# One decoder layer on one core: the mix of attention values as three passes of split values

## The chip, the cores and the metric

The kernel runs on one core of a Trainium2 chip. The metric is the device time of one execution in microseconds (us); less is better. The kernel before takes 398.93 us, the median of three runs (398.75 to 399.02).

## The reference, cut to what matters

One decoder layer for 8 sequences of 128 tokens with 512 features: a Mamba-2 mixer with a gated MLP (inner width 1792), attention of each sequence over its own context of 128 keys, and a base matrix with a routed low-rank addition. A layer norm stands behind each of the three parts.

```python
def _L0_xattn_ref(query, key):
    a = jnp.einsum('bqd,bkd->bqk', query, key)
    e = jax.nn.softmax(a, axis=-1)
    c = jnp.einsum('bqk,bkd->bqd', e, key)
    return c
x = _layernorm(x + mamba_and_mlp(x))
x = _layernorm(x + _L0_xattn_ref(x, ctx_4096))
x = _layernorm(x + _L0_ffn_ref(x, ...))
```

(The first of the three norms is abridged: `mamba_and_mlp` is the call of `_L0_attn_ref`.) The change touches only the last einsum of the attention: 128 queries by 128 keys, times 128 keys by 512 features, once for each sequence.

## The kernel before, in words

One sequence (128 tokens by 512 features) is one tile; there are 8, numbered 0 to 7. The kernel is written engine by engine, with the order of each engine's instructions by hand and with semaphores between them. No planner moves anything. It has three stages: the mixer, gate and up of the MLP, and the **down loop** (the last third of the span), the only stage that the change touches.

Large products run as **three passes**. A value in 32 bits is split into a high part, its rounding to the type fp32r (ScalarE copies it), and a low part, the value less the high part (VectorE or GpSimd subtracts). TensorE then adds high by low, high by high and low by high into one bank of PSUM, one instruction each (`three_pass`, L646 to L648). A product whose operands are plain 32-bit values is one call in the code and takes two matrix instructions in the trace.

The down loop is software-pipelined over the tiles. Each engine has a function `tail(t, par, ...)`; this text calls one pass through it **step t**. In step t TensorE works on three tiles at once, in this order:

- `down(t, ..., 0)`: the down projection of tile t, inner blocks 0 to 7, 24 instructions. Before it TensorE waits for `hid_lo` (both parts of the hidden values of tile t are there).
- `turn_x1(t-1)` (L882): four transposes of the normed result of tile t-1, after the semaphore `ln_out[0]` from VectorE.
- `turn_x2(t-2)`, two more blocks of down, `attend(t-1)` (L902, the scores), two more blocks.
- `base(t-2)` (base matrix and routing logits), `turn_ex(t-1)` (L908, transposes the exponentials), block 12 of down.
- `turn_z(t-2)` (L958), **`mix(t-1)`** (L913, the values), block 13 of down, `lora(t-2)` (L964, L966).

ScalarE in step t computes the reciprocal deviations for the norms (L1363, L1365), copies the turned tiles out of PSUM (L1373, L1377), makes the high part of the hidden values of tile t+1 (`split_hid`, L1356), then takes the exponential (`exp_scores`, L1387), copies its transpose (L1390) and copies the turned routing values (L1394).

VectorE in step t runs in this order:

- `add_mlp(t-1)` (L1846) and moments, `add_ffn(t-3)` (L1855, L1856), `normed(0, t-1)` (L1804, which releases `turn_x1(t-1)` of the next entry on TensorE's list), the third norm of tile t-3, `lo_of_x2(t-2)` (L1882)
- `row_max(t-1)` (L1893), then `route(t-2)`, seven small instructions (L1810 to L1837)
- `split_hid(t+1)` (L1791, the low part of the hidden values: releases `hid_lo`)
- `add_attention(t-1)` (L1898, L1901: waits for the mix), moments and norm of its result (L1797, L1799, L1804)

Step 0 has only down. Step 1 has no routing and no base (f is False there), step 2 has all but the third norm, and steps 3 to 6 are full; 3 to 6 are a hardware loop on TensorE and ScalarE, 5 and 6 on VectorE. Step 7, written out, is drawn together: its down projection is cut by `END_SEGS` instead of `SEGS`, so that only five blocks (15 instructions) stand ahead of `turn_x1(6)`, and four blocks behind `mix(6)`.

```python
SEGS = ((0, 8), (8, 10), (10, 12), (12, 13), (13, 14))
END_SEGS = ((0, 5), (5, 6), (6, 8), (8, 9), (9, 13), (13, 14))
```

The context of tile t comes by two DMAs into the place of its hidden values, issued by SyncE when these are split (L481, L482): the turned keys, and 512 words further the keys as they are, which serve as values.

The functions that the diff touches:

Of the kernel before, what the change touches and what calls it, by code (L numbers as in the profile page):

```python
# [132 lines left out]
def build(nc, x, ctx, ctxT, wstream, conv_w, conv_b, a_log, d_skip, dt_bias, ln1_w, ln2_w,  # L133
          gate_lora, expert_bias, lora_b, out):
    es = ExitStack()
    with es:
        def sb(name, shape, dt=F32):
            return es.enter_context(nc.sbuf_tensor(name, shape, dt))

        def sem(name):  # L140
            return es.enter_context(nc.semaphore(name))
# [7 lines left out]
        def at(name, word, shape, dt=F32):  # L149
# [25 lines left out]
                    rawS[:, 3 * CH:4 * CH].rearrange("p (s n) -> p s n", s=2))  # L175
        x2S = x2_parts[0]
        rows = sb("rows", [P, B, D])
        big = sb("big", [P, NM * TOK])
        tmp = sb("tmp", [P, 7 * D])

        sums = side[:, 0:CH]
        sg = tmp[:, 0:4 * D].rearrange("p (k n) -> p k n", k=4)
# [32 lines left out]
        x2T = tmp[:, 2560:3072]  # L215
        ex = tmp[:, 3072:3200]
        exT = tmp[:, 3200:3328]
        zm = tmp[:, 3328:3456]
        stats = tmp[:, 3456:3474].rearrange("p (k s) -> p k s", k=3)
        lg = tmp[:, 3488:3488 + 3 * E].rearrange("p (k e) -> p k e", k=3)  # L220
# [74 lines left out]
        ln_u, ln_st, ln_mv, ln_log, ln_rs, ln_out = (  # L295
            [sem(f"ln{i}_{what}") for i in (1, 2, 3)] for what in ("u", "st", "mv", "log", "rs", "out"))
        q_ps, q_ok, sc_ps, mx_ok, ex_ok = sem("q_ps"), sem("q_ok"), sem("sc_ps"), sem("mx_ok"), sem("ex_ok")
        rinv_ok, exT_ps, exT_ok, pv_ps = sem("rinv_ok"), sem("exT_ps"), sem("exT_ok"), sem("pv_ps")
        raw_max, scaled = sem("raw_max"), sem("scaled")
        x2_ps, x2_ok, x2_hi, x2_lo = sem("x2_ps"), sem("x2_ok"), sem("x2_hi"), sem("x2_lo")  # L300
# [87 lines left out]
        def base_w(part, c):  # L388

            return base_end if part * DC + c == 2 * DC - 1 else baseS[:, part * DC + c, :]  # L390

        def context(t):

# [257 lines left out]
        def _(pe):  # L651
# [255 lines left out]
                pe.wait_ge(ex_ok, t + 1)  # L907
                pe.transpose(bank[4][:, P:2 * P], ex, ident[:, :]).then_inc(exT_ps, 1)  # L908

            def mix(t):  # L910
                pe.wait_ge(exT_ok, t + 1)
                _, key = context(t)
                pe.matmul(bank[5][:, :], exT, key, start=True, stop=True).then_inc(pv_ps, 1)  # L913
# [58 lines left out]
            def tail(t, par, d=True, a=True, f=True, first_d=False, first_f=False):  # L972

                if d:
                    down(t, par, 0, first_d)
                if a:
                    turn_x1(t - 1)
                if f:
                    turn_x2(t - 2, par)
                if d:  # L980
                    down(t, par, 1, first_d)
                if a:
                    attend(t - 1, 1 - par)
                if d:
                    down(t, par, 2, first_d)
                if f:
                    base(t - 2, first_f)
                if a:
                    turn_ex(t - 1)
                if d:  # L990
                    down(t, par, 3, first_d)
                if f:
                    turn_z(t - 2)
                if a:
                    mix(t - 1)
                if d:
                    down(t, par, 4, first_d)
                if f:
                    lora(t - 2)
# [15 lines left out]
            down(last, 1, 2, False, END_SEGS)  # L1015
            turn_ex(last - 1)
            down(last, 1, 3, False, END_SEGS)
            mix(last - 1)
            down(last, 1, 4, False, END_SEGS)
            turn_x2(last - 1, 0)  # L1020
            down(last, 1, 5, False, END_SEGS)
# [13 lines left out]
            mix(last)  # L1035
# [15 lines left out]
        def _(act):  # L1051
# [315 lines left out]
            def store(t):  # L1367
                act.wait_ge(ln_out[2], t + 1)
                act.dma_start(out[bass.ds(t, 1)].rearrange("a p n -> (a p) n"), u3).then_inc(stored, 16)
# [15 lines left out]
            def exp_scores(t, scale=1.0):  # L1385
# [4 lines left out]
                act.activation(exT, bank[4][:, P:2 * P], ACT.Copy).then_inc(exT_ok, 1)  # L1390
# [6 lines left out]
            def tail(t, par, a=True, f=True, g=True, split=True, first_split=False):  # L1397

                if a:
                    rstd(0, t - 1)  # L1400
                if g:
                    rstd(2, t - 3)
                if a:
                    copy_q(t - 1)
                if f:
                    hi_of_x2(t - 2)
                if split:
                    split_hid(t + 1, 1 - par, first_split)
                if g:
                    store(t - 3)  # L1410
                if a:
                    exp_scores(t - 1)
                if f:
                    copy_z(t - 2)
                if a:
                    rstd(1, t - 1)
# [3 lines left out]
            bw_high(0)  # L1420
            bw_high(1)
            route_high()
            tail(1, 1, f=False, g=False)
            tail(2, 0, g=False)
            with act.Fori(1, B // 2 - 1) as j:
                tail(2 * j + 1, 1)
# [4 lines left out]
            copy_q(last - 1)  # L1431
            hi_of_x2(last - 2)
            store(last - 3)
            exp_scores(last - 1)
# [5 lines left out]
            exp_scores(last, scale=lrs[:, 0:1])  # L1440
            rstd(2, last - 2)
            rstd(1, last)
            copy_halves(last, x2T, x2_ps, (3, 5), x2_ok)
# [11 lines left out]
        def _(v):  # L1455
# [435 lines left out]
            def row_max(t):  # L1891
                v.wait_ge(sc_ps, t + 1)
                v.tensor_reduce(sm[:, 0:1], bank[4][:, 0:P], AX.X, ALU.max, negate=True).then_inc(mx_ok, 1)  # L1893

            def add_attention(t, par):

                v.wait_ge(ex_ok, t + 1)
                v.reciprocal(sm[:, 2:3], sm[:, 1:2]).then_inc(rinv_ok, 1)  # L1898
                v.wait_ge(rinv_ok, t + 1)
                v.wait_ge(pv_ps, t + 1)  # L1900
                v.scalar_tensor_tensor(out=u2[:, par, :], in0=bank[5][:, :], scalar=sm[:, 2:3], in1=u1,  # L1901
                                       op0=ALU.mult, op1=ALU.add).then_inc(ln_u[1], 1)

            def tail(t, par, a=True, f=True, g=True, split=True, first_g=False):

                if a:
                    add_mlp(t - 1, 1 - par)
                    moments(0, t - 1, u1)
                if g:
                    add_ffn(t - 3, 1 - par, stored_tiles=None if first_g else t - 3)  # L1910
                if a:
                    normed(0, t - 1, u1)
                if g:
                    moments(2, t - 3, u3)
                    normed(2, t - 3, u3)
                if f:
                    lo_of_x2(t - 2)
                if a:
                    row_max(t - 1)
                if f:  # L1920
                    route(t - 2)
                if split:
                    split_hid(t + 1, 1 - par)
                if a:
                    add_attention(t - 1, 1 - par)
                    moments(1, t - 1, u2[:, 1 - par, :])
                    normed(1, t - 1, u2[:, 1 - par, :])
# [19 lines left out]
            normed(2, last - 3, u3)  # L1947
            lo_of_x2(last - 2)
            row_max(last - 1)
            add_attention(last - 1, 0)  # L1950
            moments(1, last - 1, u2[:, 0, :])
            normed(1, last - 1, u2[:, 0, :])
# [84 lines left out]
```

## Time and profile before

| what | us |
|---|---|
| median of three runs | 398.93 |
| the profiled execution, its own time | 400.36 |
| its span, first to last instruction | 398.6 |
| TensorE busy in the span | 383.1 |
| VectorE busy | 293.0 |
| ScalarE busy | 191.2 |
| GpSimd busy | 135.0 |

The profile lists for each engine the start and the duration of every instruction, and where the engine was idle before it, what ended the idle time. The matrix instructions of TensorE overlap: a 512-column pass is listed with some 0.39 us, and the next one starts some 0.23 us after it. So the distance between starts is what counts there. On VectorE and ScalarE an instruction may be listed as starting slightly before its forerunner ends.

### The profile page before, as it was taken

How to read it: one execution, taken by the hardware profiler on the slowest of the kernel's cores; microseconds unless marked ns; L12 is line 12 of the kernel's file. 1: busy time of each engine (PE TensorE's matmuls, PEld its weight loads, DVE VectorE, ACT ScalarE, POOL GpSimd, SP SyncE). 2: the span in 40 equal slices, each digit the busy share in tenths (PEclk: the TensorE clock that was granted, in tenths of full speed). 3: DMA queues.
4: the chain of work that ended last, by engine and by line, in shares of the span. 5: the costliest groups of instructions: out<-in, count | busy, mean ns of one | idle time of the engine just before them, and what ended most of it. 6: DMA issues, size and time to landing. Idle time of an engine off the chain costs nothing.

```text
span 398.6 us, 5321 instructions
## 1 busy us (share of the span) xinstructions
PE 383.1 (96%) x1891; PEld 310.2 (78%) x1891; DVE 293.0 (74%) x514; ACT 191.2 (48%) x385; POOL 135.0 (34%) x121
## 2 busy tenths in 40 slices
PE   7999999999899999999999999999999999998994
PEld 3778787766579988888888888888788888896773
DVE  2589996277775888979797979696655857658587
ACT  5678465866755566152524243863234144143141
POOL 2504222844644674647382827840000000000000
PEclk9999999999999999999999999999999999999998
DMA  7801531110001023121212111352102102101002
GB/s 262 285 38 53 156 118 46 53 54 0 1 2 53 3 87 125 53 57 50 72 38 102 37 72 53 115 178 78 54 7 74 53 26 79 53 26 54 28 0 81
DMA packets 12979, 27.63 MB, mean 69 GB/s; under 512 B 1841, under 2 KB 2225, under 8 KB 12954
## 3 DMA queue, kind: packets, MB, share of 16 engines
q1 hardware_dynamic: 12090, 25.87, 19.5%
q10 hardware_dynamic: 864, 1.44, 1.0%
q8 instruction: 14, 0.23, 0.3%
q14 instruction: 11, 0.09, 0.1%
HBM read 25.20 MB, written 2.11 MB: 69 GB/s over the span
## 4 chain that ended last, share of the span: by engine, by line
PE 80%; DVE 8%; ACT 6%; POOL 3%; issue 2%; DVEq 0%; ACTq 0%; POOLq 0%
PE bank L646 23%; PE bank L648 22%; PE bank L647 22%; PE bank L762 2%; PE bank L902 2%; PE bank L913 2%; PE bank L657 1%; POOL sets L551 1%; PE bank L685 1%; DVE tmp L1797 1%; DVE big L1566 1%; ACT big L1138 1%; ACT big L1063 1%; DVE tmp L1609 1%; PE bank L918 1%
## 5 line engine op out<-in xcount | busy, mean ns | idle before, releaser
L646 PE MATMUL bank<-sets,station 128*128 128x512 f32 (+1 forms) x424 | 164.9, 389 | 2.7 <-DVE sets L1591 1.1
L647 PE MATMUL bank<-sets,station 128*128 128x512 f32 (+1 forms) x424 | 158.5, 374 | 0.0
L648 PE MATMUL bank<-sets,station 128*128 128x512 f32 (+1 forms) x424 | 158.5, 374 | 0.0
L646 PEld LDWEIGHTS bank<-sets,station 128*128 128x128 f32 x424 | 79.9, 188 | 20.0 <-issue 4.2
L647 PEld LDWEIGHTS bank<-sets,station 128*128 128x128 f32 x424 | 80.0, 189 | 14.8 <-issue 2.2
L648 PEld LDWEIGHTS bank<-sets,station 128*128 128x128 f32 x424 | 79.8, 188 | 14.6
L604 POOL TENSOR_TENSOR big<-tmp,side_f 128x512 f32<-128x512 f32 x17 | 26.4, 1567 | 23.8 <-DVE side_f L1670 23.8
L1363 ACT ACTIVATE small<-small 128x1 f32<-128x1 f32 x24 | 7.1, 296 | 50.2 <-DVE small L1799 50.2
L509 POOL TENSOR_TENSOR station<-raw,station 128x1024 fp32r<-128x1024 f32 x7 | 16.8, 2396 | 40.0 <-ACT station L1055 40.0
L1670 DVE TENSOR_TENSOR side_f<-side_f,bank 128x512 f32<-128x512 f32 x36 | 24.6, 685 | 3.9 <-PE bank L648 3.5
L1523 DVE SCALAR_TENSOR_TENSOR big<-bank,cw,big 128x508 f32<-128x508 f32 (+2 forms) x36 | 26.2, 740 | 1.4 <-ACT big L1115 0.3
L1654 DVE TENSOR_TENSOR station<-raw,station 128x512 fp32r<-128x512 f32 (+1 forms) x24 | 20.6, 898 | 6.1 <-ACT station L1254 6.1
L1670 DVE TENSOR_TENSOR tmp<-tmp,bank 128x512 f32<-128x512 f32 x30 | 20.4, 682 | 3.2 <-PE bank L648 3.2
L1254 ACT ACTIVATE station<-raw 128x512 fp32r<-128x512 f32 x12 | 7.5, 625 | 29.6 <-PE bank L648 29.6
L1664 DVE TENSOR_TENSOR station<-side_f,station 128x512 fp32r<-128x512 f32 x24 | 19.4, 813 | 3.2 <-ACT station L1277 3.2
L1277 ACT ACTIVATE station<-side_f 128x1024 fp32r<-128x1024 f32 x12 | 12.7, 1059 | 13.9 <-POOL side_f L596 13.9
L647 PE MATMUL bank<-side,rawS 128*128 128x274 f32 (+1 forms) x60 | 17.7, 296 | 0.0
L648 PE MATMUL bank<-side,rawS 128*128 128x274 f32 (+1 forms) x60 | 17.7, 296 | 0.0
L1804 DVE TENSOR_SCALAR tmp<-tmp,small 128x512 f32<-128x512 f32 x21 | 11.4, 545 | 8.4 <-ACT small L1365 8.4
L1797 DVE BATCH_NORM_STATS2 tmp<-tmp 128x6 f32<-128x512 f32 x24 | 16.6, 693 | 0.6
L591 POOL TENSOR_TENSOR side_f<-raw 128x256 f32<-128x256 f32 x12 | 9.1, 754 | 20.3 <-DVE station L1664 20.3
L1791 DVE TENSOR_TENSOR station<-big,station 128x1792 fp32r<-128x1792 f32 x7 | 14.1, 2017 | 0.0
(206 smaller groups left out, 657.8 us busy)
## 6 DMA issues: line engine op xcount, KB each, us to landing
raw<-wstream SPq DMA_DIRECT2D x31, 512.0 KB, 3.4
rows<-x SPq DMA_DIRECT2D x8, 256.0 KB, 4.5
big<-ctxT SPq DMA_DIRECT2D x8, 256.0 KB, 2.6
big<-ctx SPq DMA_DIRECT2D x8, 256.0 KB, 2.9
out<-tmp ACTq DMA_DIRECT2D x5, 256.0 KB, 2.0
decays<-step_rows SPq DMA_DIRECT2D x4, 256.0 KB, 3.5
big<-step_rows SPq DMA_DIRECT2D x4, 256.0 KB, 5.2
out<-tmp SPq DMA_DIRECT2D x2, 256.0 KB, 2.2
```

The source lines that it names most:

```text
L509: pool.tensor_tensor(dst, raw[:, raw_slot(n), :], hi.bitcast(F32), ALU.subtract).then_inc(w_lo, 1)
L604: pool.tensor_tensor(hid_block(m, hf), blocks(sg[:, k, :]), blocks(value), ALU.mult).then_inc(up_ok, 1)
L646: pe.matmul(ps, a_hi, b_lo, start=first, stop=False)
L647: pe.matmul(ps, a_hi, b_hi, start=False, stop=False)
L648: return pe.matmul(ps, a_lo, b_hi, start=False, stop=last)
L1277: act.activation(groupS[:, buf, 0, D + HALF_K:7 * HALF_K], sums, ACT.Copy).then_inc(g_hi, 1)
L1523: v.scalar_tensor_tensor(out=dst[:, :, s:L], in0=src[:, :, 0:L - s], scalar=cw[:, m, 3 - s:4 - s], in1=dst[:, :, s:L], op0=ALU.mult, op1=A ...
L1654: v.tensor_tensor(groupS[:, buf, 1, lo:hi], src, groupS[:, buf, 0, lo:hi].bitcast(F32), ALU.subtract) \
L1664: v.tensor_tensor(groupS[:, buf, 1, q], sums[:, bass.ts(k, D)], groupS[:, buf, 0, q].bitcast(F32), ALU.subtract).then_inc(g_lo, 1)
L1670: v.tensor_tensor(dst, other, product_bank(g, n), op).then_inc(done, 1)
L1791: v.tensor_tensor(hidS[:, par, 1, :], big[:, bass.ds(t * (NM * P), NM * P)], hidS[:, par, 0, :].bitcast(F32), ALU.subtract).then_inc(hid_l ...
L1797: v.bn_stats(stats[:, k, :], u).then_inc(ln_st[i], 1)
```

## The change

In steps 1 to 7 the mix of tiles 0 to 6 becomes three passes. `mix_last` is the old `mix`, for tile 7.

- ScalarE: `high_key(t-1)` copies the values (128x512) as their high part into raw slot 0, ahead of `exp_scores`. At its first use it waits until that slot is read out (`bw_lo`). The copy of the turned exponentials (L1390 before) now writes the high part of them.
- VectorE: `low_key(t-1)` behind `row_max` puts the low part of the values in place of the values themselves (128x512). `low_of_exT(t-1)` subtracts the high part from the turned exponentials in PSUM (128x128) and puts the low part where the exponentials stood; it waits for ScalarE's copy (`exT_ok`) and stands ahead of `split_hid`, behind `route` where there is one.
- TensorE: `mix` waits for `key_lo` and `exT_ok`, runs two passes, waits for `exT_lo`, and runs the third.

```diff
+            def high_key(t, par, first_use=False):
+                if first_use:
+                    act.wait_ge(bw_lo, 5)
+                act.wait_ge(ctx_in[par], 16 * (t + 2 - par))
+                _, key = context(t)
+                act.activation(key_high(par), key, ACT.Copy).then_inc(key_hi, 1)
...
+            def low_key(t, par):
+                v.wait_ge(key_hi, t + 1)
+                _, key = context(t)
+                v.tensor_tensor(key_low(t), key, key_high(par).bitcast(F32), ALU.subtract).then_inc(key_lo, 1)
+
+            def low_of_exT(t):
+                v.wait_ge(exT_ok, t + 1)
+                v.tensor_tensor(exT_parts[1], bank[4][:, P:2 * P], exT_parts[0].bitcast(F32), ALU.subtract).then_inc(exT_lo, 1)
...
                 if a:
                     row_max(t - 1)
+                    low_key(t - 1, 1 - par)
                 if f:
                     route(t - 2)
+                if a:
+                    low_of_exT(t - 1)
                 if split:
                     split_hid(t + 1, 1 - par)
...
-            def mix(t):
+            def mix(t, par):
+                pe.wait_ge(key_lo, t + 1)
+                pe.wait_ge(exT_ok, t + 1)
+                pe.matmul(bank[5][:, :], exT_parts[0], key_low(t), start=True, stop=False)
+                pe.matmul(bank[5][:, :], exT_parts[0], key_high(par), start=False, stop=False)
+                pe.wait_ge(exT_lo, t + 1)
+                pe.matmul(bank[5][:, :], exT_parts[1], key_high(par), start=False, stop=True).then_inc(pv_ps, 1)
+
+            def mix_last(t):
                 pe.wait_ge(exT_ok, t + 1)
                 _, key = context(t)
                 pe.matmul(bank[5][:, :], exT, key, start=True, stop=True).then_inc(pv_ps, 1)
...
@@ step 7, VectorE
             row_max(last - 1)
+            low_key(last - 1, 0)
+            low_of_exT(last - 1)
             add_attention(last - 1, 0)
```

`exT_parts` are the places of `exT` (high) and `ex` (low), `key_low(t)` the place of the values in the context of tile t, `key_high(par)` a half of raw slot 0.

## Rows read from the trace of the kernel before

**Rows 1.** Windows: busy us of each engine, PE clock granted, DMA share, GB/s.
```profile
319.30:335.10 15.80, 15.80 (x89) 13.44 (x88) 10.45 (x25) 5.07 (x13) 0.00 (x0) 1.00 0.14 50
...
364.00:367.00 3.00, 1.50 (x10) 1.01 (x9) 2.90 (x8) 0.50 (x2) 0.00 (x0) 1.00 0.03 10
...
394.00:398.00 4.00, 0.00 (x0) 0.00 (x0) 2.03 (x5) 0.50 (x2) 0.00 (x0) 0.73 0.37 131
```

**Rows 2.** Chain that ended last, 325 to 337 us: start, us, what.
```profile
327.96 0.86 PE bank L913 x2
328.82 0.23 PE bank L646
```

**Rows 3.** Timeline of TensorE, step 4 into 5: start, us, what.
```profile
326.88 0.27 PE L908 MATMUL bank<-ident,tmp 128*128 128x128 f32 x1
...
327.80 1.02 PE L913 MATMUL bank<-big,tmp 128*128 x2
...
329.60 0.40 PE L646 MATMUL bank<-sets,station 128*128 128x512 f32 x1
...
335.12 0.60 PE L882 MATMUL bank<-ident,tmp 128*128 128x128 f32 x4
```

**Rows 4.** Timeline of VectorE, step 4 into 5; idle before it in brackets.
```profile
325.55 0.16 DVE L1810 TENSOR_TENSOR tmp<-bank,eb 128x4 f32<-128x4 f32 x1 [2.61 <-PE bank L648]
...
326.90 0.19 DVE L1837 TENSOR_TENSOR tmp<-tmp 128x32 fp32r<-128x32 f32 x1
327.01 2.02 DVE L1791 TENSOR_TENSOR station<-big,station 128x1792 fp32r<-128x1792 f32 x1
...
331.43 0.55 DVE L1804 TENSOR_SCALAR tmp<-tmp,small 128x512 f32<-128x512 f32 x1 [0.60 <-ACT small L1365]
331.89 0.68 DVE L1846 TENSOR_TENSOR tmp<-bank,rows 128x512 f32<-128x512 f32 x1
...
334.12 0.55 DVE L1804 TENSOR_SCALAR tmp<-tmp,small 128x512 f32<-128x512 f32 x1
```

**Rows 5.** Timeline of ScalarE, step 4.
```profile
322.97 0.37 ACT L1387 ACTIVATE tmp<-bank,small 128x128 f32<-128x128 f32 x1 [0.17 <-DVE small L1893]
...
327.19 0.28 ACT L1390 ACTIVATE tmp<-bank 128x128 f32<-128x128 f32 x1 [3.75 <-PE bank L908]
```

**Rows 6.** Groups by line and form: count, busy us, mean ns.
```profile
L1888 DVE TENSOR_TENSOR rawS<-bank,rawS 128x256 fp32r<-128x256 f32 x2 | 0.8, 419 | 0.3 <-ACT rawS L1445 0.3
...
L1254 ACT ACTIVATE station<-raw 128x512 fp32r<-128x512 f32 x12 | 7.5, 625 | 29.6 <-PE bank L648 29.6
```

**Rows 7.** Line L1694: ns min/median/max, first and last start.
```profile
L1694 DVE TENSOR_TENSOR rawS<-raw,side x1: 684/684/684, 271.7 to 271.7; 128x512 fp32r<-128x512 f32 x1
```

**Rows 8.** Timeline of VectorE, step 1 into 2.
```profile
278.61 0.29 DVE L1893 TENSOR_REDUCE small<-bank 128x1 f32<-128x128 f32 x1 [3.28 <-PE bank L902]
278.82 2.02 DVE L1791 TENSOR_TENSOR station<-big,station 128x1792 fp32r<-128x1792 f32 x1
...
281.74 0.75 DVE L1901 SCALAR_TENSOR_TENSOR tmp<-bank,small,tmp 128x512 f32<-128x512 f32 x1 [0.83 <-PE bank L913]
...
286.73 0.55 DVE L1804 TENSOR_SCALAR tmp<-tmp,small 128x512 f32<-128x512 f32 x1 [0.60 <-ACT small L1365]
```

**Rows 9.** Timeline of ScalarE, step 1.
```profile
280.11 0.28 ACT L1390 ACTIVATE tmp<-bank 128x128 f32<-128x128 f32 x1 [0.71 <-PE bank L908]
```

**Rows 10.** Timeline of TensorE, steps 2 and 7.
```profile
287.64 0.60 PE L882 MATMUL bank<-ident,tmp 128*128 128x128 f32 x4
...
366.37 0.66 PE L882 MATMUL bank<-ident,tmp 128*128 128x128 f32 x4 [1.50 <-DVE tmp L1804]
...
371.42 1.02 PE L913 MATMUL bank<-big,tmp 128*128 128x512 f32 x2
```

**Rows 11.** Timeline of VectorE, step 7.
```profile
365.77 0.55 DVE L1804 TENSOR_SCALAR tmp<-tmp,small 128x512 f32<-128x512 f32 x1
...
372.55 0.75 DVE L1901 SCALAR_TENSOR_TENSOR tmp<-bank,small,tmp 128x512 f32<-128x512 f32 x1 [2.14 <-PE bank L913]
```

More of the change, by code:

```diff
@@ L177, in build @@
         rows = sb("rows", [P, B, D])
+        big_at = -(-nc.sbuf_base // 32) * 32
         big = sb("big", [P, NM * TOK])
+        bigS = nc.alloc_sbuf_tensor_at("bigS", [P, NM * TOK], F32R, offset=big_at)
+        tmp_at = -(-nc.sbuf_base // 32) * 32
         tmp = sb("tmp", [P, 7 * D])
+        tmpS = nc.alloc_sbuf_tensor_at("tmpS", [P, 7 * D], F32R, offset=tmp_at)
         sums = side[:, 0:CH]
@@ L217, in build @@
         exT = tmp[:, 3200:3328]
+        exT_parts = (tmpS[:, 3200:3328], tmpS[:, 3072:3200])
         zm = tmp[:, 3328:3456]
@@ L297, in build @@
         q_ps, q_ok, sc_ps, mx_ok, ex_ok = sem("q_ps"), sem("q_ok"), sem("sc_ps"), sem("mx_ok"), sem("ex_ok")
+        key_hi, key_lo, exT_lo = sem("key_hi"), sem("key_lo"), sem("exT_lo")
         rinv_ok, exT_ps, exT_ok, pv_ps = sem("rinv_ok"), sem("exT_ps"), sem("exT_ok"), sem("pv_ps")
@@ L390, in base_w, with key_high, key_low @@
             return base_end if part * DC + c == 2 * DC - 1 else baseS[:, part * DC + c, :]
+        def key_high(par):
+            return rawS[:, bass.ts(par, D)]
+        def key_low(t):
+            return bigS[:, bass.ds(t * (NM * P) + D, D)]
         def context(t):
@@ L994, in tail @@
                 if a:
-                    mix(t - 1)
+                    mix(t - 1, 1 - par)
                 if d:
@@ L1017, in _ @@
             down(last, 1, 3, False, END_SEGS)
-            mix(last - 1)
+            mix(last - 1, 0)
             down(last, 1, 4, False, END_SEGS)
@@ L1034, in _ @@
             base_half(0, 1, x2_parts[1], (2,))
-            mix(last)
+            mix_last(last)
             base_half(0, 1, x2_parts[1], (3,))
@@ L1383, in copy_halves, with exp_scores @@
                     act.activation(dst[:, bass.ts(i, 2 * P)], bank[banks[i]][:, 0:2 * P], ACT.Copy).then_inc(done, 1)
[L1385 removed]
+            def high_key(t, par, first_use=False):
[4 more added lines that the diff above has]
+                act.activation(key_high(par), key, ACT.Copy).then_inc(key_hi, 1)
+            def exp_scores(t, scale=1.0, last=False):
                 act.wait_ge(mx_ok, t + 1)
@@ L1389, in exp_scores @@
                 act.wait_ge(exT_ps, t + 1)
-                act.activation(exT, bank[4][:, P:2 * P], ACT.Copy).then_inc(exT_ok, 1)
+                act.activation(exT if last else exT_parts[0], bank[4][:, P:2 * P], ACT.Copy).then_inc(exT_ok, 1)
             def copy_z(t, bk=3):
@@ L1395, in copy_z, with tail @@
                     .then_inc(zmT_ok, 1)
-            def tail(t, par, a=True, f=True, g=True, split=True, first_split=False):
+            def tail(t, par, a=True, f=True, g=True, split=True, first_split=False, first_key=False):
                 if a:
@@ L1411, in tail @@
                 if a:
+                    high_key(t - 1, 1 - par, first_key)
                     exp_scores(t - 1)
@@ L1422, in _ @@
             route_high()
-            tail(1, 1, f=False, g=False)
+            tail(1, 1, f=False, g=False, first_key=True)
             tail(2, 0, g=False)
@@ L1433, in _ @@
             store(last - 3)
+            high_key(last - 1, 0)
             exp_scores(last - 1)
@@ L1439, in _ @@
             copy_z(last - 2, bk=2)
-            exp_scores(last, scale=lrs[:, 0:1])
+            exp_scores(last, scale=lrs[:, 0:1], last=True)
             rstd(2, last - 2)
```

## The prediction

> **What bounds the kernel now.** I read the windows first. In a full step of the down loop TensorE is busy for all of its 15.80 us at a granted clock of 1.00, its upper level of 2.4 GHz; VectorE is busy for 10.45 us and ScalarE for 5.07 us [rows 1]. The chain of waits agrees: between 325 and 337 us it is TensorE alone, and the old mix has 0.86 us in it, a pass of down 0.23 us [rows 2]. So a first look says: TensorE bounds, and shortening the mix pays.
>
> The second look must go to the thing that the busy shares hide, the order of VectorE's work. TensorE turns the exponentials at 326.88 and wants the normed tile for `turn_x1` at 335.12 [rows 3]. Between these lies a chain on ScalarE and VectorE. VectorE finishes the routing at 327.09 (326.90 + 0.19) and works through twelve instructions, from the split of the hidden values at 327.01 to the norm that ends at 334.67 (334.12 + 0.55), idle only for the 0.60 us of the deviation that ScalarE computes; `add_mlp` at 331.89 waits for nobody [rows 4]. A norm is handed to TensorE in 0.05 us: in step 7 it ends at 366.32 [rows 11], and the transposes start at 366.37 [rows 10]. So in a full step VectorE is early by only 335.12 - 334.67 - 0.05 = 0.40 us. In step 7, where five blocks of down stand ahead of `turn_x1` and not eight, TensorE already waits 1.50 us for it [rows 10]: VectorE has no room there at all. What the change does to this chain decides the time.
>
> **TensorE: the mix.** It goes from 0.86 us to three passes of 0.23 us, 0.70 us with rounding, as passes behind one another run everywhere here [rows 2]. That saves 0.16 us in each of seven mixes. Ends: nothing, if the waits inside hold it up; 0.17 us, if they don't. The wait for `exT_lo` should not: the mix starts at 327.80 [rows 3], its third pass is due 0.46 us later, at 328.26, and the subtraction ends by 327.79 (next part). In steps where TensorE then waits for VectorE the saving is worth nothing, since the chain starts at `turn_ex`, which stands ahead of the mix.
>
> **ScalarE: the high part of the values.** 128x512 from SBUF takes 0.63 us [rows 6]. It stands behind the split of the hidden values and ahead of the exponential, which was waiting 0.17 us at 322.97 [rows 5]; the exponential comes some 0.4 us later, and `turn_ex` is not due before 326.88 [rows 3], so 3 us cover it. Cost 0; without this cover, 0.4 us a step. The values have landed by then, since the scores of the same tile, from the same pair of DMAs, were already taken. In step 1 the slot is free, as VectorE was done with the base weights before its first norm. No DMA is added or moved; the copy of the turned exponentials only changes its target type.
>
> **VectorE: the low part of the values.** 128x512 takes 0.68 us [rows 7]. In a full step VectorE is idle for 2.61 us ahead of the routing [rows 4], so it costs 0. In step 7 it falls into the wait for the mix, 2.14 us [rows 11]: 0. In step 1 it stands ahead of a wait that is longer anyway (below).
>
> **VectorE: the low part of the exponentials.** This is the expensive edit. Not its length: 128x256 from PSUM takes 0.42 us [rows 6], so 128x128 is some 0.29 us, and as neighbours overlap by 0.08 us (326.90 + 0.19 against 327.01 [rows 4]), 0.21 us from start to start. It is the wait in front of it. It needs ScalarE's copy, which ends at 327.19 + 0.28 = 327.47 [rows 5], while VectorE could start the split of the hidden values at 327.01. Behind the waiting instruction stand the split, the attention sum, three norms: all of the chain above. The split now starts at 327.47 + 0.03 + 0.21 = 327.71, 0.70 us late.
>
> A rule of the Trainium skill speaks further against it ("VectorE: DVE Perf Modes", The DRAIN you can't avoid): a VectorE instruction does not start before the pipe of the one ahead is empty, so one should count instructions and not semaphores. The row shows an overlap of 0.08 us at this very place [rows 4], so I do not charge the drain in full; by the rule it would.
>
> Now the sum, by the place where TensorE waits.
>
> - Steps 3, 4, 5 and 6 (behind the mixes of steps 2 to 5): VectorE is 0.70 us late against a room of 0.40 us, so `turn_x1` is 0.30 us late, four times: 1.20 us. The split ends at 329.73 as well, later than TensorE wants it for the first block of down (329.60 [rows 3], now 0.16 earlier). It waits there about 0.3 us, and the 24 passes that follow then reach `turn_x1` at about 335.3, just ahead of the norm at 335.42. These two waits are one, not two.
> - Step 2 (behind step 1): there is no routing in step 1, so before, the split started at 278.82, directly after the row maximum. It now waits for the copy of the turned exponentials, which ends at 280.39 [rows 9], and starts at 280.63: 1.81 us late. Of this 0.80 us is taken up by the time that VectorE stood waiting for the mix (0.83 less a usual gap of 0.03 [rows 8]), which leaves 1.01. The norm ended at 287.28 [rows 8], `turn_x1` began at 287.64 [rows 10]: room 0.31. Cost 0.70 us.
> - Step 7 (behind step 6): no room. Cost 0.70 us.
> - The mix of step 7: VectorE waited for it (2.14 us) and what follows waits for VectorE [rows 11]. Behind `turn_ex` of step 7 the low part of the exponentials is done by the third pass, as above: the mix starts at 371.42 [rows 10], its saving counts. -0.16 us.
>
> Together 0.70 + 1.20 + 0.70 - 0.16 = 2.44 us. A TensorE that has been kept waiting needs a little to start: the four transposes take 0.66 us after a wait and 0.60 us without [rows 10, 3]. That is up to 0.06 us at five new waits, 0.30 us together. I take the middle: +2.6 us. The profiled execution (400.36 us, span 398.6) would become about 403.0 with a span of 401.2; on the median of 398.93 us it makes **401.5 us**.
>
> Ends: if the subtraction starts and ends 0.1 us sooner at each of six places and no start-up is paid, +1.84. If each of the six costs its full length and another 0.1 us of handover, with start-up, 2.74 + 6 x 0.18 = +3.8. So this case has 400.8 to 402.7.
>
> **The rivals.**
>
> - The pipe's drain is paid in full. The split then starts 0.08 us later at six places, +0.5 us: 402.0 us. Against it: the overlap in rows 4, between two small instructions. For it: the subtraction is larger than these. This is the rule of the skill's page named above.
> - TensorE keeps the bound and the mix pays everywhere: 7 x 0.16 = 1.1 us less, 397.8 us, on the other side of no change. The mechanism is the room at `turn_x1`: it decides at a delay of 0.40 us of the split in full steps. Only if more than 0.70 us of VectorE's chain could be made up does it hold; for it speaks that TensorE was at 100% [rows 1] and the chain of waits names no other engine [rows 2]; against it the twelve instructions with only 0.60 us of idle time [rows 4].
> - Half of it: if the copy of the turned exponentials were ready by the end of the routing (0.38 us sooner than in rows 5), the delay would be only 0.21 us; full steps would gain 0.16 each and the other terms eat that, within 0.5 us of no change: 399.2 us.
> - Only the ends cost: the full steps absorb the delay, steps 2 and 7 do not. +0.70 + 0.70 - 0.16 = 1.24, 400.2 us.
> - The three passes don't do what they should, because the wait for `exT_lo` holds the third: then the mix of step 7 gains nothing, and 401.7 us result. The margin of 0.47 us speaks against it.
> - TensorE's clock falls in the longer waits. In step 7 the idle time grows from 1.50 to 2.2 us. With 1.50 us idle in a stretch of 3 us the granted clock stayed 1.00; it fell to 0.73, part of the stretch at the lower level of 1.2 GHz, where TensorE had nothing for 4 us at the end [rows 1]. If it fell in step 7, the 5 us of work up to the mix would take up to twice as long: 406 us.
>
> **How the numbers follow.** Chances: the forecast 0.65, the drain 0.12, the ends only 0.06, the mix without a gain 0.03, the clock 0.03, TensorE keeps the bound 0.06, the half case 0.05. Faster by over 0.2% (0.8 us, about what can be told from no change) is then 0.06, within it 0.05, slower 0.89. The range reaches from 400.5, a little below the likeliest case's own low end, to 402.8; the ends-only case, the clock and the cases on the other side lie outside, with 0.2.
>
> **What would show it.** Right: VectorE idle about 0.4 us behind L1837 until ScalarE's copy in steps 2 to 6, and about 1 us or more in step 1; new waits of TensorE of 0.2 to 0.4 us for `hid_lo` or `ln_out` in each step from 2 to 6; 2.2 us instead of 1.50 at `turn_x1` in step 7; full steps of 16.1 us and not 15.8; the three passes 0.23 us apart. Wrong: full steps of 15.8 us or less, no wait of TensorE in them, or the subtraction beginning before the routing.

## The result, and the profile after

The changed kernel takes 402.46 us (median of four runs, 401.82 to 402.99) against 398.84 us before (median of four, 398.53 to 399.02): slower by 3.6 us, ratio 1.008 (95% interval 1.0058 to 1.0103). The forecast was 401.5 us in a range of 400.5 to 402.8.

In single executions of every kernel here, changed or not, the start of the kernel is short or some 2 us longer (the first transposes of the down loop begin near 273.8 or near 275.6 us), so profiles are compared from these transposes on, and not by their spans.

From there to the last instruction the kernel before takes 398.6 - 275.69 = 122.9 us and the changed one 400.5 - 273.64 = 126.9 us. Of the 3.95 us of difference, 2.7 us are those of the forecast, term by term (see the point-by-point account below). The rest, 1.2 us, is a fall of TensorE's clock in step 7, a rival to which I had given a chance of 0.03.

First VectorE of the changed kernel, step 4 into 5 (columns: start, us, what, idle time before it and what ended it). L1868 is the end of the routing, L1933 the new subtraction, L1822 the split of the hidden values, L1835 the norm; they answer to [rows 4].

```profile
326.34 0.19 DVE L1868 TENSOR_TENSOR tmp<-tmp 128x32 fp32r<-128x32 f32 x1
326.94 0.29 DVE L1933 TENSOR_TENSOR tmpS<-bank,tmpS 128x128 fp32r<-128x128 f32 x1 [0.41 <-ACT tmpS L1419]
327.15 2.02 DVE L1822 TENSOR_TENSOR station<-big,station 128x1792 fp32r<-128x1792 f32 x1
...
334.25 0.55 DVE L1835 TENSOR_SCALAR tmp<-tmp,small 128x512 f32<-128x512 f32 x1
```

The routing ends at 326.53 and the split starts at 327.15. Before, it overlapped the routing's end by 0.08 us [rows 4]. So it is 0.70 us late: 0.41 us of pure waiting and 0.29 us for the subtraction. TensorE in the same step, which answers to [rows 3]:

```profile
326.32 0.27 PE L922 MATMUL bank<-ident,tmp 128*128 128x128 f32 x1
...
327.13 0.27 PE L980 MATMUL bank<-ident,tmp 128*128 128x128 f32 x1
327.16 0.49 PE L927 MATMUL bank<-bigS,tmpS 128*128 x1
327.49 0.40 PE L928 MATMUL bank<-rawS,tmpS 128*128 128x512 f32 x1
327.73 0.40 PE L930 MATMUL bank<-rawS,tmpS 128*128 128x512 f32 x1
327.96 0.40 PE L660 MATMUL bank<-sets,station 128*128 128x512 f32 x1
328.19 0.39 PE L661 MATMUL bank<-sets,station 128*128 128x512 f32 x1
...
329.22 0.50 PE L660 MATMUL bank<-sets,station 128*128 128x512 f32 x1 [0.17 <-DVE station L1822]
...
334.86 0.66 PE L896 MATMUL bank<-ident,tmp 128*128 128x128 f32 x4
```

The same two neighbours of the mix in the kernel before, `turn_z` ahead of it and the second pass of the block behind it (starts of the passes right beside the old mix are listed unevenly, so I take these):

```profile
327.69 0.27 PE L958 MATMUL bank<-ident,tmp 128*128 128x128 f32 x1
...
328.89 0.40 PE L647 MATMUL bank<-sets,station 128*128 128x512 f32 x1
```

The three passes (L927, L928, L930) run without a gap, and the third does not wait. Between the two neighbours it is 328.19 - 327.13 = 1.06 us, before 328.89 - 327.69 = 1.20 us: 0.14 us saved, where 0.16 was forecast. The saving is real, and TensorE then gives it away twice. At 329.22 it waits for the split of the hidden values: from the second pass of the block to this pass it is 1.03 us (329.22 - 328.19), before 0.71 (329.60 - 328.89), 0.32 us more. And its transposes take 0.66 us instead of 0.60, the mark of having waited. From turned exponentials to `turn_x1` it is 8.54 us, before 8.24 [rows 3].

Windows of step 7 (length, then busy us of PE, PEld, DVE, ACT, POOL, then the granted clock, DMA share and GB/s), and TensorE's marks there, which answer to [rows 10]:

```profile
362.00:365.00 3.00, 3.00 (x15) 2.37 (x13) 2.33 (x5) 0.50 (x2) 0.00 (x0) 1.00 0.53 171
365.00:368.00 3.00, 1.06 (x8) 0.78 (x7) 2.88 (x8) 0.50 (x2) 0.00 (x0) 0.96 0.03 10
368.00:371.00 3.00, 3.00 (x13) 2.71 (x12) 1.24 (x2) 2.10 (x5) 0.00 (x0) 0.50 0.24 90
371.00:374.00 3.00, 3.00 (x16) 2.42 (x15) 1.25 (x4) 0.73 (x3) 0.00 (x0) 0.97 0.00 0
```

```profile
361.59 0.50 PE L660 MATMUL bank<-sets,station 128*128 128x512 f32 x1 [0.17 <-DVE station L1822]
...
367.22 0.66 PE L896 MATMUL bank<-ident,tmp 128*128 128x128 f32 x4 [1.94 <-DVE tmp L1835]
...
372.74 0.27 PE L922 MATMUL bank<-ident,tmp 128*128 128x128 f32 x1
```

The wait ahead of `turn_x1` grew from 1.50 to 1.94 us. That is less than the 0.76 us by which the step became longer, because TensorE comes to it later as well: at 361.59 it has already waited for the split of the hidden values. Behind the 1.94 us a window of three microseconds ran at 0.50 of full speed, 1.2 GHz, TensorE's lower level; the windows around it were granted 0.96 and 0.97, so that the lower level lasted a little over 3 us. From `turn_x1` to `turn_ex` it is 5.52 us; before, 4.25 (366.37 to 370.62).

### The profile page after: what moved, and what is told of

It reads as the page before. It is cut to its first block, busy times and chain, and to the rows that moved or that the text cites. A ratio compares the mean times of both kernels' runs of the same rounds, so it can differ in the third digit from the quotient of the medians.

```text
span 400.5 us, 5370 instructions
## 1 busy us (share of the span) xinstructions
PE 382.5 (95%) x1898; PEld 310.9 (78%) x1898; DVE 299.4 (75%) x528; ACT 193.9 (48%) x392; POOL 134.9 (34%) x121
## 4 chain that ended last, share of the span: by engine, by line
PE 75%; DVE 11%; ACT 6%; POOL 3%; issue 3%; DMA 1%; SPq 0%; DVEq 0%; ACTq 0%; POOLq 0%
PE bank L660 23%; PE bank L662 22%; PE bank L661 22%; DVE station L1822 3%; PE bank L916 2%; DMA rows<-x 1%; POOL sets L565 1%; ACT big L1085 1%; DVE big L1597 1%; PE bank L699 1%; PE bank L896 1%; PE bank L940 1%; DVE tmp L1828 1%; DVE tmp L1640 1%; PE bank L671 1%
## 5 line engine op out<-in xcount | busy, mean ns | idle before, releaser
L1835 DVE TENSOR_SCALAR tmp<-tmp,small 128x512 f32<-128x512 f32 x21 | 11.4, 544 | 8.4 <-ACT small L1387 8.4
L1822 DVE TENSOR_TENSOR station<-big,station 128x1792 fp32r<-128x1792 f32 x7 | 14.1, 2015 | 0.0
```

The source lines that it names most:

```text
L1822: v.tensor_tensor(hidS[:, par, 1, :], big[:, bass.ds(t * (NM * P), NM * P)], hidS[:, par, 0, :].bitcast(F32), ALU.subtract).then_inc(hid_l ...
```

## The experiments

All times of a kernel are medians. Ratios are against the kernel before in the same round, estimated over the executions, and are not the quotient of the two medians. The table (us) is worked out from the starts of the four transposes `turn_x1` in each profiled execution: "step 2" is the distance from those of step 1 to those of step 2, and so on. "Rest" reaches from those of step 7 to the end of the span, "down loop" from the first of them to the end. In the last row the transposes of steps 1 to 6 stand one block (0.70 us) later than in the others.

| kernel | step 2 | steps 3 to 6, mean | step 7 | rest | down loop |
|---|---|---|---|---|---|
| before | 11.95 | 15.82 | 15.43 | 32.2 | 122.9 |
| changed | 12.64 | 16.19 | 16.19 | 33.3 | 126.9 |
| changed, again | 12.64 | 16.19 | 16.20 | 32.0 | 125.6 |
| changed, filled wait | 12.65 | 16.20 | 16.18 | 32.0 | 125.7 |
| before, filled wait | 11.94 | 15.82 | 15.43 | 32.2 | 122.9 |
| subtraction alone, waiting | 12.65 | 16.18 | 16.18 | 32.2 | 125.8 |
| subtraction alone, not waiting | 11.94 | 15.82 | 15.64 | 32.2 | 123.0 |
| two passes | 11.70 | 15.50 | 15.50 | 33.0 | 122.2 |
| two passes, filled wait | 11.69 | 15.48 | 15.47 | 31.8 | 120.9 |
| split ahead of the transposes | 12.44 | 15.80 | 15.42 | 32.4 | 123.4 |
| GpSimd, behind the transposes | 12.84 | 16.86 | 16.29 | 32.0 | 128.6 |
| GpSimd, ahead of them | 11.95 | 15.77 | 15.44 | 32.4 | 122.8 |
| changed, one block more | 12.97 | 16.07 | 15.42 | 32.0 | 124.7 |

### Is it the subtraction behind ScalarE's copy? (the kernel before, plus that instruction)

```diff
             if a:
+                low_of_exT(t - 1)     # waits for exT_ok; its result is not used
             if split:
                 split_hid(t + 1, 1 - par)
```

> The kernel before, with nothing added but the subtraction behind the copy of the turned exponentials (low_of_exT, at the place on VectorE where the change has it). The mix stays as it was; the result of the subtraction is used by nobody. Theory W (the wait on VectorE is the whole cause): the same losses as in the changed kernel, 0.7 us in step 2, 0.36 in each of steps 3 to 6, 0.76 in step 7, without the 0.16 us that the mix of step 7 gains: +2.9 us, 401.8; and 403.0 if the clock falls in step 7 as well, since its wait grows to 2.2 us. Rival K (the high and low parts of the values, or the three passes, cost time): clearly less than +2.9, for instance +1.

Measured: 401.38 us, ratio 1.0082 (1.0068 to 1.0096). The step times are those of the changed kernel within 0.03 us. One VectorE instruction of 0.29 us at this place accounts for everything that the change costs; the parts of the values and the three passes are not in this kernel. Theory K falls. The clock did not fall in its profiled execution, though its wait in step 7 was as long (1.95 us).

### Is it the wait or the work? (the same instruction between constants)

```diff
+            def same_work():
+                v.tensor_tensor(spare, ident[:, :], ident[:, :], ALU.subtract)   # 128x128, waits for nobody
```

> The kernel before, with one VectorE subtraction of 128x128 added where the change has low_of_exT, but between constants: it waits for nobody and its result is not used. It is the counterpart of low_only, which waits. Theory W: 0.21 us from start to start; full steps have a room of 0.40 us and stay at 15.82, step 2 stays at 11.95, step 7's norm comes 0.21 us later: +0.2 us in all. Rival B (VectorE's work at this place is what counts, or its drain): full steps longer by 0.1 us or more, +0.7 us and above; low_only measured +2.9 for the same instruction with its wait.

Measured: 399.67 us, ratio 1.0021 (1.0002 to 1.004). The median lies inside the scatter that the start makes (its executions run from 398.42 to 400.85); the profile is clear: full steps of 15.82 us as before, step 7 0.21 us longer, as forecast. VectorE of this kernel:

```profile
324.86 0.19 DVE L1838 TENSOR_TENSOR tmp<-tmp 128x32 fp32r<-128x32 f32 x1
324.97 0.28 DVE L1897 TENSOR_TENSOR rawS<-ident 128x128 fp32r<-128x128 f32 x1
325.18 2.02 DVE L1792 TENSOR_TENSOR station<-big,station 128x1792 fp32r<-128x1792 f32 x1
```

The instruction costs 0.21 us from start to start, and the room of 0.40 us takes it. With its wait the same instruction costs 0.70 us, which the room does not take. So of the 2.9 us by which the down loop of the waiting form is longer (125.8 against 122.9), 2.7 are the wait (125.8 against 123.0). The two also differ in what they read, a bank of PSUM or a constant, but the instruction lasts 0.29 and 0.28 us.

### The change without the low part of the exponentials

```diff
-                pe.matmul(bank[5][:, :], exT_parts[0], key_high(par), start=False, stop=False)
-                pe.wait_ge(exT_lo, t + 1)
-                pe.matmul(bank[5][:, :], exT_parts[1], key_high(par), start=False, stop=True).then_inc(pv_ps, 1)
+                pe.matmul(bank[5][:, :], exT_parts[0], key_high(par), start=False, stop=True).then_inc(pv_ps, 1)
...
-                    low_of_exT(t - 1)
```

> The changed kernel without low_of_exT and without the third pass of the mix; so the product leaves out the low part of the exponentials. The high and low parts of the values stay. Theory W: VectorE does not wait for ScalarE's copy any more, TensorE saves 0.86 - 0.47 = 0.39 us in each mix, and VectorE's room of 0.40 us just covers that: full steps of 15.43 us, 0.25 to 0.4 us less up to step 2, nothing for step 7's norm (it is VectorE's), 0.39 us less behind the mix of step 7: -2.2 us, 396.6. If the clock falls in step 7, where the wait becomes 1.9 us, 397.9. Rival K: if the parts of the values cost time, full steps stay near 15.8 us or above, and the time near 398.8.

Measured: 396.76 us, ratio 0.9959 (0.9938 to 0.9981). Full steps of 15.50 us where 15.43 were expected: TensorE saves 0.39 us and VectorE's room is just used up. The transposes take 0.66 us and not 0.60, the mark of a short wait. A saving up to this room is thus passed on: 0.33 us a step. The high and low parts of the values (0.63 us on ScalarE, 0.68 us on VectorE in each step) are in it and cost nothing. In the profiled execution the clock fell in step 7, as the second branch of the expectation had it.

### The clock: the wait of step 7 filled

```diff
             down(last, 1, 0, False, END_SEGS)
+            keep_warm(5, 4, wd(0, 0)[:, 0:P], wd(0, 0))
             turn_x1(last - 1)
```

> The changed kernel with five more matrix instructions (128x512, into a bank that nobody reads then) on TensorE ahead of turn_x1 in step 7, in the wait that is 1.94 us long there. Nothing else is changed. Theory C (the clock): in the trace of the changed kernel the granted clock falls to 0.50 right behind this wait, and the stretch from turn_x1 to turn_ex of step 7 takes 5.52 us instead of 4.25. With the wait mostly filled (5 x 0.23 = 1.15 us) the clock stays at 1.00, the stretch takes 4.25 us again, and the time falls by 1.2 to 1.3 us, to about 401.2. Rival N (the fall comes from elsewhere, or the profiled execution was a chance): no difference, 402.5. Rival L (the longer stretch is a queue or the new subtraction): the clock stays up, but the stretch keeps its 5.5 us.

Measured: 401.46 us, ratio 1.0087 (1.0073 to 1.01). From `turn_x1` to `turn_ex` of step 7 it takes 4.25 us again, with the clock at 1.00. But this alone proves little, as the unaltered kernel shows next, in another round.

> The changed kernel once more, unaltered, in the same round of measurements as the three others. Until now, single executions show two things that come and go: the clock's fall in step 7 (1.27 us where it comes), and a start of the kernel that is 2 us longer (the first transposes of the down loop begin at 275.6 us and not at 273.7). Theory C: the step 7 fall comes in some executions and not in others; executions then cluster near 401.3 (no fall; 398.5 + 2.75 by the steps of the trace) and near 402.5 (fall), and the clusters, not a spread, make the difference between the 402.46 measured first and the 401.4 of low_only and after_warm. Rival: one cluster at 402.4 only; then the filling of after_warm saves 1 us in every execution, and low_only's 401.38 needs another cause.

Measured: 401.49 us, ratio 1.0059 (1.0037 to 1.008). Its profiled execution, with the same wait of 1.93 us and nothing to fill it, kept its clock:

```profile
366.00:369.00 3.00, 1.55 (x11) 1.31 (x11) 2.33 (x8) 1.22 (x5) 0.00 (x0) 1.00 0.01 3
369.00:372.00 3.00, 2.93 (x18) 2.38 (x17) 1.94 (x4) 1.84 (x5) 0.00 (x0) 1.00 0.24 90
```

Its down loop is 1.2 us shorter than in the first profile of the very same code (125.6 against 126.9), and that difference lies wholly behind `turn_x1` of step 7. So the fall comes in some executions and not in others. Five profiled executions have a wait of 1.88 to 1.95 us there with nothing to fill it: it came in two of them (changed 1.94, two passes 1.88) and not in three (changed again 1.93, subtraction alone 1.95, one block more 1.93). Six of the eight executions of this second round lie between 401.2 and 401.7 us, where the forecast of the steps puts them. The theory had expected a second group near 402.5 as well; only one run (403.04) is above 401.9, so in this round the fall was rare or absent.

> two_passes (the low part of the turned exponentials and its pass are left out) with the five filling instructions. Its profiled execution had both a long start and the fall in step 7 and took 399.6; most others took 396.5. Theory C: the fall of 1.26 us can't come any more: executions at 396.5, and with the long start at about 398.4, none at 399.6. Rival: the filling changes nothing and 399.6 comes again.

Measured: 397.04 us, ratio 0.9946 (0.9926 to 0.9965). Here the filling can be judged by its executions: without it three of twelve took 399.6 to 399.7 us, with it none of twelve is above 398.4. The profile shows the long start and the fall together for one of the three; the four highest with the filling, 398.3 to 398.4, stand where a long start without a fall was expected. That the filling keeps the clock up is likely by this and not shown: the two were measured in different rounds, on different chips. The windows of both, the unfilled first, both profiled with the long start:

```profile
362.00:365.00 3.00, 1.12 (x6) 0.63 (x5) 2.93 (x7) 0.50 (x2) 0.00 (x0) 1.00 0.02 5
365.00:368.00 3.00, 3.00 (x15) 2.71 (x14) 1.71 (x4) 2.10 (x5) 0.00 (x0) 0.55 0.15 58
```

```profile
362.00:365.00 3.00, 2.27 (x12) 1.61 (x11) 2.93 (x7) 0.50 (x2) 0.00 (x0) 1.00 0.04 11
365.00:368.00 3.00, 2.93 (x21) 2.38 (x19) 1.91 (x6) 2.10 (x5) 0.00 (x0) 1.00 0.17 65
```

> The kernel before with the same five filling instructions ahead of turn_x1 in step 7. The control for after_warm. Its wait there is 1.50 us and its clock did not fall in the profile. Theory C: no difference from before, 398.5 (within 0.2); it also can't be slower, since 5 x 0.23 us fit into the wait. Rival: the clock falls in part of its executions as well (some were near 400.3), then the filling removes those and the highest times go, while the median stays.

Measured: 398.66 us, ratio 0.9994 (0.9974 to 1.0014): no difference, as expected for a wait of 1.50 us behind which the clock had not fallen. The filling itself costs nothing that can be seen.

### The same VectorE work, ahead of the transposes

ScalarE rounds the exponentials in SBUF, VectorE subtracts directly behind `low_key`, both parts are turned, and one ScalarE instruction copies both.

```diff
+            def low_of_ex(t):
+                v.wait_ge(exh_ok, t + 1)
+                v.tensor_tensor(ex.bitcast(F32R), ex, exh, ALU.subtract).then_inc(exl_ok, 1)
...
                     low_key(t - 1, 1 - par)
+                    low_of_ex(t - 1)
...
-                    low_of_exT(t - 1)
```

> All three passes, and VectorE does the same two subtractions as in the changed kernel, but the one for the exponentials (128x128) before they are turned: ScalarE rounds them in SBUF, VectorE subtracts directly behind low_key, in its idle time ahead of the routing; TensorE turns both parts (one transpose of 0.11 us more), and ScalarE copies both out in one instruction. So there is no VectorE instruction behind ScalarE's copy. Theory W (the wait in front of the subtraction is the cost, not the work): VectorE's chain from the routing on is as in the kernel before, full steps of 15.82 - 0.16 + 0.11 = 15.77 us, the total 0.3 us below before, 398.2; VectorE is about as busy as in the changed kernel. Rival B (VectorE's added busy time is the cost, wherever it stands): full steps of 16.1 to 16.2 us and 401.3. If the clock falls in step 7, 1.3 us more in either case.

Measured: 399.59 us, ratio 1.0016 (0.9998 to 1.0034). VectorE executes as many instructions as in the changed kernel (528, busy for 299.6 against 299.4 us), and full steps are 15.8 us and not 16.2. So in full steps its added busy time is free; theory B falls. The forecast of 398.2 was too low all the same. By the table the down loop is 0.5 us above before, where 0.3 below was forecast, and the trace shows where:

```profile
280.10 0.30 PE L932 MATMUL bank<-ident,raw 128*128 128x128 f32 x1 [0.24 <-DVE tmp L1957]
...
327.56 0.39 ACT L1443 ACTIVATE rawS<-bank 128x256 fp32r<-128x256 f32 x1 [3.30 <-PE bank L932]
...
328.05 0.27 PE L992 MATMUL bank<-ident,tmp 128*128 128x128 f32 x1
328.19 0.49 PE L938 MATMUL bank<-bigS,rawS 128*128 x1
```

In step 1, where VectorE has no idle time, TensorE now waits for the subtraction (step 2: 0.49 us longer than before). In full steps the first pass starts 0.14 us after `turn_z`, where 0.03 is usual, which eats the rest of the saving. That it waits for the copy of both parts is argued and not shown: the copy is listed as ending at 327.95, 0.24 us ahead of the pass, but the delay is gone in the version with GpSimd ahead of the transposes (below), where the high part is copied alone. Behind the transposes of step 7 another 0.14 us are lost (32.37 against 32.23).

### GpSimd in VectorE's place

GpSimd does the subtraction in steps 1 to 6, on a second copy that ScalarE makes; the filling stands in step 7.

```diff
+                if pooled:
+                    act.activation(ex, bank[4][:, P:2 * P], ACT.Copy).then_inc(ex_raw, 1)
...
+            for t in range(B - 2):
+                pool.wait_ge(exT_ok, t + 1)
+                pool.wait_ge(ex_raw, t + 1)
+                pool.tensor_tensor(exT_parts[1], ex, exT_parts[0].bitcast(F32), ALU.subtract).then_inc(exT_lo, 1)
```

> The changed kernel with the low part of the turned exponentials moved from VectorE to GpSimd in steps 1 to 6 (GpSimd has nothing to do in this stage). As GpSimd is not given PSUM, ScalarE makes a second, unrounded copy into SBUF for it (128x128, about 0.2 us more). In step 7 VectorE still does it. The filling instructions of after_warm stand in step 7. Theory W: VectorE is back in its old rhythm, so nothing is late at turn_x1; the mixes save 0.16 us each in steps 1 to 5 and 7: -0.96 us against before, 397.9. It needs GpSimd's subtraction to be done by the third pass: copies end at 327.66 on the old time axis, a subtraction of 128x128 by 128x512 in 1.30 us is about 0.4 to 0.5 us, the pass is due at 328.2: at the edge. If it is 0.1 to 0.2 us late in each step, the mixes save nothing, 398.8. Rival K (the parts of the values or more work on the other engines cost time): above 398.8.

Measured: 404.38 us, ratio 1.0167 (1.0148 to 1.0187), the slowest of all, where 397.9 was forecast and 398.8 for a GpSimd at the edge. The split of the hidden values follows the routing again without a wait, but TensorE waits 0.95 us at the third pass:

```profile
329.01 1.56 POOL L646 TENSOR_TENSOR tmpS<-tmp,tmpS 128x128 fp32r<-128x128 f32 x1 [15.28 <-ACT tmp L1426]
```

```profile
328.24 2.02 DVE L1829 TENSOR_TENSOR station<-big,station 128x1792 fp32r<-128x1792 f32 x1
```

```profile
329.28 0.40 PE L932 MATMUL bank<-rawS,tmpS 128*128 128x512 f32 x1
330.63 0.50 PE L934 MATMUL bank<-rawS,tmpS 128*128 128x512 f32 x1 [0.95 <-POOL tmpS L646]
```

The third pass starts 1.35 us behind the second and not 0.23. Together with its slow start (0.33 us to the next pass and not 0.23), less the 0.16 us of the mix, that is 1.06 us; full steps are 1.04 us longer than before. So the size of one estimate failed: the subtraction was taken at 0.4 to 0.5 us and takes 1.56 (1.32 in step 1).

GpSimd's instruction stands beside VectorE's split, which reads two tensors of SBUF until 330.26, and ends 0.31 us after it. In step 1, where it begins later in the split, it takes 1.32 us and again ends 0.31 us behind (280.29 against 279.98). The Trainium skill, "SBUF — State Buffer" (SBUF: two separate sides), has this as a rule: a VectorE instruction with two SBUF inputs and a GpSimd instruction that reads SBUF take one pair of ports in turn, whole instructions at a time. The next run agrees: ahead of the transposes, away from the split, a GpSimd instruction of the same size takes 0.46 us.

```profile
324.49 0.46 POOL L649 TENSOR_TENSOR tmp<-tmp,raw 128x128 fp32r<-128x128 f32 x1 [15.32 <-ACT raw L1436]
```

> A version to beat both, with all three passes. As early_split, but GpSimd makes the low part of the exponentials, ahead of the transposes and not beside VectorE's long split; the two parts are turned into two banks and copied one by one, so that the first pass does not wait for both (in early_split it waited 0.11 us in each step); and step 1 keeps the old mix, since VectorE has no idle time there. Theory W: full steps of 15.77 us, nothing late in steps 2 and 7, 0.05 us less in each of six steps: 0.3 us below before, 398.1 to 398.2. If GpSimd is late (it waits beside VectorE as in pool_low, where 128x128 took 1.56 us), TensorE has 3 us of other work first, so that should cost nothing. Rival: a new wait at the transposes or at the second copy takes the 0.05 us back, 398.5.

This is the version with GpSimd ahead of the transposes. Its core is `pool.tensor_tensor(ex.bitcast(F32R), ex, exh, ALU.subtract)` in place of `low_of_ex`, a second PSUM bank for the turned low part, and the old mix in step 1. Measured: 398.9 us, ratio 1.0004 (0.9983 to 1.0024): no difference that can be told, where 398.1 to 398.2 was forecast. By the profile full steps are 15.77 us, exactly as forecast, 0.05 us below before; step 7 gives 0.14 us back, so the down loop stands 0.06 us below before. It has all three passes and none of the loss, but no gain either.

### More room at the transposes

```diff
-SEGS = ((0, 8), (8, 10), (10, 12), (12, 13), (13, 14))
+SEGS = ((0, 9), (9, 10), (10, 12), (12, 13), (13, 14))
```

> The changed kernel with SEGS = ((0, 9), (9, 10), ...): one more block of down (0.70 us) stands ahead of turn_x1 in steps 0 to 6, one fewer behind it. VectorE's chain now has 0.40 + 0.70 us of room there. Theory W with two waits at one price: the norm is covered, but the split of the hidden values still ends at 329.7 on the old axis and TensorE wants it at 329.4, so it waits about 0.3 us for hid_lo; full steps of about 16.05 us instead of 16.19 (15.66 if that wait did not exist, 16.19 if the room at turn_x1 did not matter). Step 7 has its own list and is unchanged. In all 0.5 to 0.7 us below the changed kernel, 400.8 against its 401.4.

Measured: 402.56 us, ratio 1.0076 (1.0046 to 1.0106), lowest 400.81; the long start is in most of its executions. The forecast was 400.8. Full steps are 16.07 us, forecast 16.05: of the 0.36 us lost against before, only 0.12 are back. The wait for the split of the hidden values takes the place of the wait for the norm, which is what the forecast says in "these two waits are one". The gain of the whole was over-estimated, as step 2 became longer by 0.33 us. In step 1 only one block now stands between `turn_x1` and the scores, which begin at 277.60, 0.05 us behind the end of ScalarE's copy of the turned tile (277.55); from the scores to the turned exponentials it is 2.45 us (277.60 to 280.05), without the extra block 2.29 (275.46 to 277.75). Step 1 of this kernel:

```profile
276.95 0.60 ACT L1395 ACTIVATE tmp<-bank 128x512 f32<-128x512 f32 x1 [2.25 <-PE bank L896]
...
277.60 0.60 PE L916 MATMUL bank<-big,tmp 128*128 128x128 f32 x3
...
280.05 0.33 PE L922 MATMUL bank<-ident,tmp 128*128 128x128 f32 x1
```

Counted with the block that its mark is late, the down loop is some 0.3 us shorter than the changed one without a fall, not 0.5 to 0.7.

## Why the prediction was right, point by point

- The mix itself: forecast 0.16 us, found 0.14 by its neighbours; the third pass doesn't wait. In the total it shows only behind the mix of step 7: the rest of the kernel takes 32.05 us in the second profile of the changed kernel (399.5 - 367.45) against 32.23, that is -0.18.
- High and low parts of the values: forecast 0, found 0 (two passes).
- Low part of the exponentials: 0.70 us late, forecast and found to the hundredth. Full steps +0.36 us each (forecast 0.30 and up to 0.06 for starting again; the upper end is right), step 2 +0.69 (0.70), step 7 +0.76 (0.70; I had not charged the start-up there). Together 0.69 + 4 x 0.36 + 0.76 - 0.18 = 2.7 us, against a forecast of 2.44 to 2.74.
- Two of the signs were read wrongly, without an effect on the sum. The idle time of VectorE in step 1 is 0.66 us and not 1 or more, since the low part of the values (0.69 us) stands ahead of it. And the wait at `turn_x1` in step 7 is 1.94 us and not 2.2: I had added the delay of the norm and left out that TensorE itself arrives later. The waits for `hid_lo` are 0.32 us by the starts in a full step, as forecast.
- The drain as a rival: the subtraction ends at 327.23 and the split starts at 327.15, an overlap of 0.08 us as in [rows 4], and without a wait the instruction costs 0.21 us from start to start and not its 0.29. In full the drain would have made the sum 0.5 us too high. I had weighed the Trainium skill's rule ("VectorE: DVE Perf Modes", The DRAIN you can't avoid) without the exception that the same section makes, that a next instruction which is not held starts earlier. The trace agrees with the exception.
- The clock as a rival: the mechanism came true in the profiled execution of the first round, and the chance of 0.03 was too low. I had one row with 1.50 us idle and no fall and one with 4 us and a fall, and put 2.2 us at the harmless end without a reason. Its price was over-estimated: not 5 us but 1.27, as the lower level lasted only a little over 3 us.
- The measured 3.6 us lie above the 2.7 us of the steps. In the second round the medians are 2.65 us apart (401.49 against 398.84). How much of the first round's excess is the clock is shown for its profiled execution only; for its other three runs it is argued from their times (401.82 to 402.99). That the first median of 402.46 us lies in the range is in part luck: the upper end of 402.8 was made of longer instructions and handovers, which did not come, and not of the clock, which fell.

What stays open: what decides whether the clock falls behind a wait of 1.9 us. The changed kernel, the same code, did both.

## What to carry to other kernels

Before shortening work on the busiest engine, look for the chain on the other engines that runs beside it and subtract: here TensorE was 100% busy and its partner only 0.40 us early. A saving was worth something only up to that room (two passes), and a delay of 0.70 us in the partner, 0.41 of it waiting, turned seven savings of 0.16 us, 1.1 us in all, into a loss of 2.7 us. A cheap instruction is expensive where it has to wait and everything behind it on its engine waits too (0.70 us in each step here); the same amount of work in the idle time ahead of an event that the engine waits for anyway was free, and cost 0.49 us in the one step that had no such idle time. And two ends of one wait (`hid_lo` and the norm) must both be given room, or one replaces the other.

## What the runs showed of the hardware that was not expected

- TensorE's clock fell to its lower level behind idle times of 1.9 us in two profiled executions (the changed kernel and the two passes, 1.94 and 1.88 us) and did not in three others (1.93 us in the same code, 1.95 and 1.93 us in two more kernels); behind 1.50 us it was not seen. Where it fell, a little over 3 us ran at 1.2 GHz, and the stretch became 1.27 us longer.
- A GpSimd subtraction of 128x128 takes 0.46 us alone (six times) and 1.56 us (five of six times, 1.32 once) beside a VectorE instruction with two SBUF inputs; VectorE was not slowed (2.02 us in both).
- After a wait, four transposes take 0.66 us and not 0.60; this small cost returned at each new wait of TensorE and made the difference between 0.30 and 0.36 us a step.
